# A graph transformer layer on one core: the second expert's share added on chip instead of by an accumulating store

## The reference

```
x = x + gnn(xn, src, dst) + mix(xn)
top_w, top_i = top_k(softmax(router(layernorm(x))), 2)
routing_weights = softmax(top_w)
expert_out = relu(relu(f @ w1 + b1) @ w2 + b2) @ w3 + b3      # f = layernorm(x), for each of 6 experts
out = x + sum(expert_out[top_i] * routing_weights)            # two terms per row
```

## Time and profile before

| | |
|---|---|
| median of 3 runs | 1755.12 us |
| profiled execution | 1756.04 us, its span 1754.3 us |
| PE busy | 1433.3 us, 82% |
| DVE busy | 1334.7 us, 76% |
| POOL busy | 609.1 us, 35% |
| POOL's indirect stores into the output (L938) | 108 times, 1336 ns each in the mean |
| DMA | 102.22 MB, mean 58 GB/s |
| granted TensorE clock over the span | 0.926 |

### The profile page before, as it was taken

One profiled execution on the slowest core, in us unless ns is written; L12 is line 12 of the kernel. 1 busy time (PEld: TensorE's weight loads), 2 busy tenths in 40 slices (PEclk: granted clock), 3 DMA queues, 4 the chain that ended last, 5 costly groups with the idle time before them and its releaser, 6 DMA issues.

```text
span 1754.3 us, 39979 instructions
## 1 busy us (share of the span) xinstructions
PE 1433.3 (82%) x12059; PEld 1340.0 (76%) x12059; DVE 1334.7 (76%) x3949; ACT 809.6 (46%) x1983; POOL 609.1 (35%) x612
## 2 busy tenths in 40 slices
PE   0147787646569999999999999999999849999997
PEld 0136777635459899898998989988899749999996
DVE  8999689899957777777777777777777646666665
ACT  1124445335625444444444444444444425555554
POOL 1564556554411222222222222222222233335555
PEclk9868789767779999999999999999999969999999
DMA  7100000003343110111101011011110154544553
GB/s 184 11 1 1 1 1 1 1 18 121 117 136 90 46 36 33 49 35 45 36 33 49 35 45 36 33 49 35 45 36 33 43 180 137 139 125 80 88 91 57
DMA packets 71138, 102.22 MB, mean 58 GB/s; under 512 B 13790, under 2 KB 53579, under 8 KB 70823
## 3 DMA queue, kind: packets, MB, share of 16 engines
q1 hardware_dynamic: 50726, 57.78, 11.9%
q0 software_dynamic: 20352, 43.71, 9.1%
HBM read 45.34 MB, written 57.47 MB: 59 GB/s over the span
## 4 chain that ended last, share of the span: by engine, by line
PE 63%; issue 13%; DVE 13%; POOL 6%; ACT 2%; DMA 2%; DVEq 1%; POOLq 0%; SPq 0%; ACTq 0%
PE turned L1374 18%; PE front L1374 16%; PE turned L1356 10%; DVE sort_mem L1674 7%; POOL acc_mem L768 5%; PE turned L1515 4%; PE front L1515 4%; PE front L1535 4%; ACT a_ring L1112 2%; DVE acc_mem L2083 1%; PE front L1403 1%; PE turned L1508 1%; PE front L1396 1%; DVE sort_mem L1682 1%; DMA gath_mem<-in_dst 1%
## 5 line engine op out<-in xcount | busy, mean ns | idle before, releaser
L1782 DVE TENSOR_TENSOR sort_mem<-lane_bf,sort_mem 128x512 bf16<-128x512 bf16 x1372 | 498.1, 406 | 204.0 <-PE turned L1356 186.6
L1112 ACT ACTIVATE a_ring<-turned 128x512 fp32r<-128x512 f32 (+2 forms) x686 | 371.0, 545 | 458.9 <-PE turned L1356 443.5
L1374 PE MATMUL front<-y_all,a_ring 128*128 128x258 f32 x2352 | 376.0, 297 | 36.2 <-ACT a_ring L1112 36.2
L1374 PE MATMUL turned<-y_all,a_ring 128*128 128x258 f32 x2450 | 387.3, 296 | 9.6 <-ACT a_ring L1112 9.6
L1374 PEld LDWEIGHTS front<-y_all,a_ring 128*128 128x128 f32 x2352 | 305.8, 190 | 43.2 <-ACT a_ring L1112 43.0
L1674 DVE TENSOR_TENSOR sort_mem<-sort_mem 128x320 f32<-128x320 f32 (+2 forms) x568 | 329.9, 642 | 3.0
L1374 PEld LDWEIGHTS turned<-y_all,a_ring 128*128 128x128 f32 x2450 | 317.3, 190 | 13.8 <-issue 10.5
L1356 PE MATMUL turned<-sort_mem 128*128 128x128 bf16 (+1 forms) x2695 | 258.7, 217 | 2.0 <-DVE sort_mem L1782 1.9
L938 POOL DMA_INDIRECT out_rows<-base x108 | 144.2, 1336 | 178.8 <-DVE base L2094 113.5
L1356 PEld LDWEIGHTS turned<-sort_mem 128*128 128x128 bf16 x2695 | 147.5, 98 | 36.2 <-DVE sort_mem L1782 2.8
L1313 PE MATMUL turned<-ident,sort_mem 128*128 128x128 f32 x286 | 62.6, 393 | 108.2 <-DVE sort_mem L1674 107.5
(11 more groups left out here) (252 smaller groups left out, 2090.2 us busy)
## 6 DMA issues: line engine op xcount, KB each, us to landing
base<-token_lists SPq DMA_DIRECT2D x54, 258.0 KB
base<-token_lists SPq DMA_DIRECT2D x54, 130.0 KB
gated_rows<-tab_mem SPq DMA_DIRECT2D x49, 128.5 KB, 3.0
late_mem<-mixed_rows SPq DMA_DIRECT2D x49, 128.0 KB
mixed_rows<-base SPq DMA_DIRECT2D x12, 512.0 KB, 3.4
feat_mem<-in_L_ffn_expert_w SPq DMA_DIRECT2D x18, 256.0 KB, 5.7
base<-in_x SPq DMA_DIRECT2D x1, 3136.0 KB
base<-in_x SPq DMA_DIRECT2D x1, 2352.0 KB
```

The source lines that it names most:

```text
L1112: nc.scalar.activation(a_ring[:, k % 2, :, :].rearrange("p s n -> p (s n)")[:, 0:width], ps_a[k % 2][:, 0:width], ACT.Copy).then_inc(S["a_ ...
L1374: last = nc.tensor.matmul(ps_agg[odd], a_ring[:, k % 2, n, :], y_part(t, part), start=(t == 0 and part == 0), stop=(t == BLOCKS - 1 and pa ...
L1782: nc.vector.tensor_tensor(hot[:, k % 2, 0:pairs, 0:lanes, :], lane_bf[:, 0:lanes, :].unsqueeze(1).broadcast_to([P, pairs, lanes, 2]), edge ...
```

## The change

In the first pass the plain stores no longer go to the output but to a new DRAM tensor of the same row layout, `first_shares`. In the second pass POOL fetches the first shares of each tile back with an indirect DMA into the place of x in the tile's slot, DVE adds the second share to them with the same instruction as in the first pass, and POOL stores the sum into the output with a plain indirect store. So the accumulating stores (54) are gone, 54 fetches are new, and the stores stay 108 in number.

A fetch is issued four tiles ahead of the store that it stands beside (AHEAD = 4), after the tile's ids have been loaded (tok_loaded). The first four fetches stand between the passes, behind the wait for all stores of the first pass. DVE waits for a tile's fetch (first_in) before it finishes the tile. The last turn of POOL's loop is written out, because the last four tiles have no fetch to issue.

```diff
+        first_in = [sem(f"first_in{s}") for s in range(PACK_SLOTS)]
-            def store_share(m, s, adding):
+            def store_share(m, s, to, last_row):
                 pool.wait_ge(S["out_ready"], m + 1)
                 pool.nop().then_inc(S["slot_free"], 1)
-                nc.gpsimd.indirect_dma_start(out=out, out_offset=id_of(s), in_=tok[:, s, X2_AT:X2_AT + DIM], in_offset=None,
-                                             bounds_check=NODES - 1, oob_is_err=False,
-                                             compute_op=ALU.add if adding else ALU.bypass).then_inc(tok_stored[s], 16)
+                nc.gpsimd.indirect_dma_start(out=to, out_offset=id_of(s), in_=tok[:, s, X2_AT:X2_AT + DIM], in_offset=None,
+                                             bounds_check=last_row, oob_is_err=False).then_inc(tok_stored[s], 16)
+
+            def fetch_share(i, s):
+                row = s % FFN_SLOTS
+                pool.wait_ge(tok_loaded[row], 16 * (FFN_UNROLL // FFN_SLOTS * i + s // FFN_SLOTS) + 16)
+                pool.nop().then_inc(S["slot_free"], 1)
+                nc.gpsimd.indirect_dma_start(out=tok[:, row, X2_AT:X2_AT + DIM], out_offset=None, in_=first_shares, in_offset=id_of(row),
+                                             bounds_check=BLOCKS * P - 1, oob_is_err=False).then_inc(first_in[s % PACK_SLOTS], 16)
...
-                    store_share(FFN_UNROLL * i + s, s % FFN_SLOTS, False)
+                    store_share(FFN_UNROLL * i + s, s % FFN_SLOTS, first_shares, BLOCKS * P - 1)
             for s in range(FFN_SLOTS):
                 pool.wait_ge(tok_stored[s], 16 * firsts * trips)
-            with nc.gpsimd.Fori(firsts, 2 * firsts) as i:
+            for s in range(AHEAD):
+                fetch_share(firsts, s)
+            with nc.gpsimd.Fori(firsts, 2 * firsts - 1) as i:
                 for s in range(FFN_UNROLL):
-                    store_share(FFN_UNROLL * i + s, s % FFN_SLOTS, True)
+                    fetch_share(i, s + AHEAD)
+                    store_share(FFN_UNROLL * i + s, s % FFN_SLOTS, out, NODES - 1)
...
                 dve.wait_ge(S["out_ps"], m + 3)
+                if k:
+                    dve.wait_ge(first_in[s % PACK_SLOTS], 16 * (FFN_UNROLL // PACK_SLOTS * i + s // PACK_SLOTS - FFN_TILES // PACK_SLOTS) + 16)
...
-                if k == 0:
-                    nc.vector.scalar_tensor_tensor(own, tok[:, row, 0:DIM], share, own, ALU.mult, ALU.add).then_inc(S["out_ready"], 1)
-                else:
-                    nc.vector.tensor_scalar(own, tok[:, row, 0:DIM], share, None, ALU.mult).then_inc(S["out_ready"], 1)
+                nc.vector.scalar_tensor_tensor(own, tok[:, row, 0:DIM], share, own, ALU.mult, ALU.add).then_inc(S["out_ready"], 1)
```

More of the change, by code:

```diff
@@ L235, in batch_under, with gps_layer @@
     return None if end <= 0 else (end - 1) // (DIM * MIX_TILES)
-def gps_layer(nc, a, out, y_table, kept_keys, mixed_rows, token_lists):
+def gps_layer(nc, a, out, y_table, kept_keys, mixed_rows, token_lists, first_shares):
     with ExitStack() as ctx:
@@ L945, in _ @@
                 for s in range(FFN_UNROLL):
-                    store_share(FFN_UNROLL * i + s, s % FFN_SLOTS, False)
+                    store_share(FFN_UNROLL * i + s, s % FFN_SLOTS, first_shares, BLOCKS * P - 1)
             for s in range(FFN_SLOTS):
                 pool.wait_ge(tok_stored[s], 16 * firsts * trips)
-            with nc.gpsimd.Fori(firsts, 2 * firsts) as i:
+            for s in range(AHEAD):
+                fetch_share(firsts, s)
+            with nc.gpsimd.Fori(firsts, 2 * firsts - 1) as i:
                 for s in range(FFN_UNROLL):
-                    store_share(FFN_UNROLL * i + s, s % FFN_SLOTS, True)
+                    fetch_share(i, s + AHEAD)
+                    store_share(FFN_UNROLL * i + s, s % FFN_SLOTS, out, NODES - 1)
+            for s in range(FFN_UNROLL):
+                if s + AHEAD < FFN_UNROLL:
+                    fetch_share(2 * firsts - 1, s + AHEAD)
+                store_share(FFN_UNROLL * (2 * firsts - 1) + s, s % FFN_SLOTS, out, NODES - 1)
         @block.scalar
@@ L2129 @@
     token_lists = nc.dram_tensor("token_lists", (TOP * SEGMENTS * SEGMENT, TOKEN), F32, kind="Internal").ap()
+    first_shares = nc.dram_tensor("first_shares", (BLOCKS * P, DIM), F32, kind="Internal").ap()
     mixed_rows = nc.dram_tensor("mixed_rows", (BLOCKS * P, DIM), F32, kind="Internal").ap()
-    gps_layer(nc, aps, out, y_table, kept_keys, mixed_rows, token_lists)
+    gps_layer(nc, aps, out, y_table, kept_keys, mixed_rows, token_lists, first_shares)
     result = run_bass_kernel_spmd(nc, [arrays], core_ids=[0])
```

## The result

The changed kernel takes 1772.58 us in the median (four runs, 1764.68 to 1775.53), the kernel before 1753.79 us beside it on the same chip: a ratio of 1.0115, 95% interval 1.0081 to 1.015. The forecast was 1756.1 us with a range to 1764, and "no change" was its likeliest case. The change makes the kernel slower by 1.15%.

A forecast was written before the change was run, and what follows sets the result against it. PE was taken to bound both passes. Border 0.6, DVE's pause at tile 72 0.1 and the end 0.3 summed to +1.0 us, on the median of 1755.12 giving 1756.1 us; range 1752.5 to 1764.

The forecast's parts named there:

- "no change": Whole kernel: PE stays the bound, with small changes at the border and end, all within 0.2% (3.5 us); chance 0.72.
- the "faster" rival: Adding stores cost something hidden; without them 1753 us, a gain over 3.5 us needing something no row shows; chance 0.06.
- "PE stays the bound: cost 0": Second pass, steady part: POOL's two indirect DMAs, 2.58 us a tile, fit PE's 2.87 us, so nothing is lost.
- "only a late part of the instruction is held": POOL in the second pass: DVE's copy holds only about the second half of an indirect DMA, until 0.13 us after it.
- The row at 1652.83: Earlier trace: a POOL DMA took its normal 1.56 us although a copy covered 1653.08 to 1654.17; cited against full blocking.
- "0.6 us to spare": Second-pass tile layout: two POOL DMAs, one held by the copy, fit each 2.87 us with about 0.6 us left.
- the milder form of my first rival: Second pass: a 1252 ns fetch and a held store pass PE's tile time by 0.1 to 0.2 us: 1761 to 1766.
- my first rival: Second pass: POOL becomes the bound; heavy form 3.67 us a tile, about 1791 us; chance 0.17, a third of it heavy.
- DVE's wait for the fetch: Second pass, steady part: fetch issued four tiles (11.5 us) ahead, transfer 2 to 3 us, so the wait is met.
- The border: Between the passes: tile 54 waits for its fetch, four-tile lead in weights hides about 4.2 us, PE loses 0.6 us.
- The end: Last store: 1.0 us earlier without a backlog, 0.8 to 1.0 later with two DMAs of backlog; taken as +0.3 us.
- the case without a backlog: Kernel's end: last store starts 0.86 us after DVE's last share and lands 2.1 to 2.5 us later, 1.0 us earlier.

The follow-up runs named there:

- e1: The changed kernel without the fetches and DVE's wait for them, leaving 54 plain stores for 54 adding ones; ratio 1.0034 to the kernel before, passes 307.1 us.
- e6: The changed kernel without fetch or waits for one, each second-pass store issued twice, the second into a spare table; ratio 1.0102 to the kernel before.
- e2: The changed kernel with DVE's copies of weights left out in the second pass; ratio 1.017 to the kernel before, passes 346.7 us.
- e12: The kernel without fetches plus a POOL addition of 128x256 values behind each second-pass store; ratio 1.0025 to the kernel before, passes 309.0 us.
- e16: The kernel with doubled second-pass stores, but the second of each pair a plain POOL DMA to fixed rows; ratio 1.0001 to the kernel before.
- e14: The change for even slots alone (5 tiles in 9), the others keeping the adding store; ratio 0.9993 to the kernel before, passes 308.5 us.
- e9: The kernel without fetches, second-pass store issued twice for even slots alone (1.56 indirect DMAs a tile); ratio 0.9994 to the kernel before.
- e4: The changed kernel with each fetch replaced by a second plain store to a spare table; ratio 1.0155 to the kernel before, passes 332.5 us.
- e3: The changed kernel with fetches issued one tile ahead instead of four; ratio 1.0211 to the kernel before, passes 343.2 us.
- e5: The changed kernel with POOL waiting on ScalarE's turned tokens instead of the load's semaphore, fetches three tiles ahead; ratio 1.011 to the kernel before.
- e8: The changed kernel fetching only 128 of 256 columns, 512 bytes a row instead of 1024; ratio 1.0124 to the kernel before, passes 324.8 us.
- e11: The kernel with doubled second-pass stores, the second of each pair moving 32 rows instead of 128; ratio 1.009 to the kernel before.

## Why the prediction was wrong

**The bound before** The earlier trace rows was read rightly: PE fills both passes, and e1 shows that the adding stores hid nothing in the two passes (the "faster" rival falls: 307.1 against 307.3 us).

**The failing step is "PE stays the bound: cost 0" in the steady part.** It rested on a sum over POOL alone, 2 x (0.99 + 0.30) = 2.58 us under 2.87. It was wrong twice.

First, as a sum. I read the earlier trace rows as "only a late part of the instruction is held", and that a held one ends 0.13 us after the copy. Both rows are true, but the rule isn't. A DMA that a copy catches within its first 0.5 us does end 0.12 to 0.13 us after it; one over which a copy starts later isn't held at all (18 such in e6, 19 in the change, none over 1.03 us long); and one that starts under a copy is held far longer. In e6's timeline above the copy runs until 1665.25; the DMA that starts under it, at 1664.48, takes 1.63 us and ends 0.86 us after the copy. It makes almost no headway until the copy is over. The row at 1652.83 is an adding store; the last one of the kernel takes 1.55 us too, so it says nothing about how long a plain one takes under a copy. So the "0.6 us to spare" of my layout was wrong: its third DMA starts at +1.72 and the copy at +1.78, and 0.06 us later it would have started under the copy and ended 0.86 after it. In the change the pair takes 3.09 us in the mean instead of 2.87. That has the sign of the milder form of my first rival, which I priced at 1761 to 1766 and gave about 0.11; the measured time lies above it.

Second, and shown by the experiments, as a theory. The rival had the right sign and not the mechanism: POOL's time is not what decides. With the copies gone (e2) POOL has 0.22 us to spare in each tile and the kernel is slower; with POOL busier but its second instruction an addition (e12) or a plain DMA (e16), PE is full. What the second pass loses by is a link that I had costed at nothing, the signals from PE to ACT and DVE. They come late when POOL issues two indirect DMAs a tile.

The doubled store alone does most of it. In e6 the passes lose 11.4 us and the end behind them 5.6, together 17.0; in the change the passes lose 20.8 and the end wins 1.4, together 19.4. The ratios, 1.0102 (1.007 to 1.0134) and 1.0115 (1.0081 to 1.015), do not tell the two apart. Within the passes the change loses more than e6, some 1 us of it at the border (e14: 308.5, e9: 307.5). The rest is not taken apart, and it isn't the direction of the fetch: with a store in its place (e4) the passes lose 25.2 us. POOL's lag behind DVE, which delays the reload of slots, is a candidate; it was argued and not tested.

Two sentences of the forecast drew on the Trainium skill. Its section "A bandwidth-pool intuition that's wrong" (SBUF — State Buffer) says that a GpSimd DMA is blocked until shortly after VectorE's copy ends. For a DMA that a copy caught in its first 0.5 us the traces agree (0.12 to 0.13 us after it); one that started under a copy ended 0.85 to 0.92 us after it, nearly its full length of 0.99. The section "Who interferes with whom", by which the second of the two blocks fully, was the better reading of that hold, and I set it aside on one row.

**DVE's wait for the fetch** was met in the steady part, as forecast: the only long one is tile 54's.

**The border.** Timeline of the kernel after:

```profile
1595.55 1.05 POOL L946 DMA_INDIRECT base<-first_shares,base  x1 [2.18 <-issue]
...
1598.29 0.42 DVE L2105 TENSOR_TENSOR base<-front,acc_mem 128x256 f32<-128x256 f32 x1 [4.00 <-DMA base<-first_shares,base]
...
1600.48 1.13 PE L1529 MATMUL turned<-sort_mem,acc_mem 128*128 128x128 f32 x8 [0.30 <-DVE acc_mem L2097]
...
1603.28 1.57 POOL L939 DMA_INDIRECT out_rows<-base  x1 [0.30 <-issue]
```

The fetch starts at 1595.55 (I had 1595.15) and the bias add at 1598.29 (1597.55). PE lacks 1.03 of 20 us in 1590 to 1610, where I had 0.6. The mechanism, that four tiles of weights hide the wait, holds, and e14 fits the size: in the same 20 us PE lacks 0.94 us in e14 and nothing in e9, and the passes are 1.0 us longer. The first store comes at 1603.28 instead of 1601.6, since two of the five fetches were held.

**The end** needs no term for a backlog. It came 1.4 us earlier, where I had +0.3. DVE, slowed by late signals, had let POOL catch up; that this is the reason is argued, and in e6 POOL did not catch up.

```profile
1763.36 0.99 POOL L939 DMA_INDIRECT out_rows<-base  x1 [1.07 <-issue]
1765.22 0.98 POOL L939 DMA_INDIRECT out_rows<-base  x1 [0.87 <-DVE base L2109]
1767.08 0.98 POOL L939 DMA_INDIRECT out_rows<-base  x1 [0.87 <-DVE base L2109]
```

The last two stores start 0.87 us after the share, as I had for the case without a backlog, and the last one lands 2.1 us after its start; the adding store before it took 2.7.

**What stays open.** Why an indirect DMA of POOL holds up PE's signals, and almost PE's alone (of the signals on these traces none of ACT is late and at most seven of DVE), no run shows. That signals of finished matmuls are held is shown by the burst in e2; whether every late one is of that kind, the modelled ends can't tell. It isn't their bytes, rows, direction, semaphores or waits. Nor is it a fixed place within POOL's instruction: late signals arrive during the DMAs, in the gaps between them, and in e2 also while POOL is idle. And it is not settled why e3 loses twice as much as e5 with the same number of DMAs (ratios 1.0211 and 1.011; e2's 1.017 lies between them, with intervals that overlap e5's), nor how far the lengths in the last row of the table vary from one execution to the next.

## What to carry to other kernels

Before a change gives GpSimd a second indirect DMA per step of a loop that TensorE bounds, count them per tile and not only add up POOL's time: here 1.56 in each 2.87 us cost no time that could be told, and 2 cost 8 to 23% of the pass, also where they fitted POOL's time (e2). If a change like this must be made, do it for a part of the tiles, or make every second DMA a plain one. When engines wait for a matmul that the timeline shows as done ("remote", or a bias add 3 us behind its matmuls), suspect the signalling, and look at what else runs beside it. And a resource that seems full is only the bound if relieving it helps; e2 showed that here it does not.

## What the runs showed of the hardware

- PE's completion signals normally come 0.3 to 0.4 us after the start of the group's last matmul. With two indirect DMAs a tile on POOL 26 to 60% of the recorded ones are late, mostly by 0.6 to 4 us; held ones can then arrive together, in e2 five within 0.28 us (1631.39 to 1631.67), though 2.9 us lie between the starts of their matmuls.
- An indirect DMA costs POOL about 1 us, nearly whatever it moves: without a copy beside it 128 rows take 0.99 to 1.02 us, of 1024 or of 512 bytes (e8), and 32 rows 0.88 (e11). A plain DMA of the same 128 KB takes 0.58 us, in the mean with copies 666 ns (e16).
- An indirect DMA that starts under DVE's copy of 128x1796 values ends 0.85 to 0.92 us after the copy (e6 and the change); one that the copy catches within 0.5 us of its start ends 0.12 to 0.13 us after it; a copy that starts later over it (0.54 us or more) doesn't hold it.
- A tensor operation of POOL beside DVE's works the other way: in e12 DVE's share took 861 ns instead of 487, and its copy 1578 instead of 1126 (e12 and e9, 1660 to 1700 us). DVE was busy for 39.50 of 40 us, and PE still lost nothing in these 40 us; the two passes took 309.0 us, 1.9 more than in e1.

```profile
L2097 DVE COPY acc_mem<-feat_mem 128x1796 f32 x15 | 23.7, 1578 | 0.0
L2107 DVE SCALAR_TENSOR_TENSOR base<-base 128x256 f32<-128x256 f32 x14 | 12.1, 861 | 0.5
```

- Stores that only write come in packets of mostly 4096 bytes, the adding ones in packets of 1024: in 120 us of the second pass the changed kernel's indirect DMAs had 2344 packets of 4096 bytes, those of the kernel before 5212 of 1024.
